# Odd state tiles scaled on ScalarE, added in pairs by adding DMAs; gate and output weights in the expert ring

## The reference

```
x = x + layernorm(mamba(layernorm(x)))      # both directions
x = x + layernorm(moe(layernorm(x)))

branch (once forward, once on the reversed sequence, 512 channels e, 16 states n):
  u     = silu(causal_conv4(x @ W_in[:ED].T))
  delta = softplus(u @ Wx_delta @ Wdt + b_dt);   B, C = u @ Wx_B, u @ Wx_C
  h[t,e,n] = exp(-delta[t,e] * exp(A_log[e,n])) * h[t-1,e,n] + delta[t,e] * B[t,n] * u[t,e]
  y[t,e]   = sum over n of C[t,n] * h[t,e,n]  + D[e] * u[t,e]
mamba = 0.5 * (y_forward + y_backward) * silu(x @ W_in[ED:].T) @ W_out.T

moe: softmax router over 8 experts, top 2; each expert and one shared one:
  gelu(x @ w1 + b1) @ w2 + b2, 256 -> 512 -> 256
```

## Time and profile before

| | |
|---|---|
| median of 3 runs | 4418.58 us (4412.04 to 4423.32) |
| profiled execution, its only recorded time: the span | 4422.2 us |
| PE / DVE / ACT / POOL busy | 3604.0 / 3788.5 / 3101.8 / 3504.8 us |
| mean granted TensorE clock | 0.895 of full speed |
| DMA traffic | 705.06 MB, 159 GB/s over the span |
| chain that ended last, by engine | DVE 29%, PE 25%, POOL 16%, issue 15%, ACT 11% |

### The profile page before, as it was taken

The page is one execution under the profiler, slowest core; times in us unless marked ns, Lnnn a source line. Parts: engine busy times, 40 slices in busy tenths (PEclk is TensorE's granted clock), DMA queues, the critical chain, the costliest instruction groups (busy, mean ns, idle before and its releaser), DMA issues.

```text
span 4422.2 us, 57941 instructions
## 1 busy us (share of the span) xinstructions
PE 3604.0 (81%) x18192; PEld 2562.9 (58%) x18192; DVE 3788.5 (86%) x4688; ACT 3101.8 (70%) x5179; POOL 3504.8 (79%) x2085
## 2 busy tenths in 40 slices
PE   4767596888879887798878887798987989788877
PEld 1444454666546655567555774556655665567656
DVE  3999999898998989899898988989999898989710
ACT  4667576787767876688766887678876787668543
POOL 3898887888878888788887888878887888878611
PEclk7878697999979999899879998899998999889988
DMA  6233142556435663357433674345743565336555
GB/s 196 91 107 104 69 150 75 191 183 214 155 104 172 205 210 130 105 182 245 153 124 131 197 238 147 125 151 194 230 141 107 179 220 188 130 113 204 167 167 182
DMA packets 375805, 705.06 MB, mean 159 GB/s; under 512 B 31937, under 2 KB 205514, under 8 KB 371530
## 3 DMA queue, kind: packets, MB, share of 16 engines
q1 hardware_dynamic: 363210, 667.79, 46.0%
q0 software_dynamic: 12288, 33.57, 2.3%
HBM read 529.82 MB, written 171.44 MB: 159 GB/s over the span
## 4 chain that ended last, share of the span: by engine, by line
DVE 29%; PE 25%; POOL 16%; issue 15%; ACT 11%; DMA 3%; SPq 1%; DVEq 0%; POOLq 0%; ACTq 0%
DVE h L1396 10%; POOL drive L1895 9%; DVE h L1393 7%; DVE y L1405 6%; PE h_t L1170 5%; PE side L1204 4%; PE side L1341 4%; PE side L1333 3%; ACT decay L1610 2%; POOL y L1913 2%; POOL xs_dram L1970 2%; DMA expert_w<-in_w 1%; PE side L1318 1%; DVE stats L1450 1%; POOL work L1982 1%
## 5 line engine op out<-in xcount | busy, mean ns | idle before, releaser
L1895 POOL TENSOR_TENSOR drive<-xu,b_row 128x1024 f32<-128x1024 f32 x960 | 2262.7, 2362 | 386.5 <-DVE h L1396 238.8
L1610 ACT ACTIVATE decay<-delta,neg_a 128x512 f32<-128x512 f32 x2048 | 1401.8, 692 | 747.0 <-DVE h L1396 424.5
L1170 PE MATMUL h_t<-ident,h 128*128 128x128 f32 x8192 | 1332.0, 301 | 523.4 <-DVE y L1405 253.4
L1170 PEld LDWEIGHTS h_t<-ident,h 128*128 128x128 f32 x8192 | 1060.1, 155 | 979.1 <-DVE y L1405 373.1
L1405 DVE SCALAR_TENSOR_TENSOR y<-h_t,c_col,y 128x512 f32<-128x512 f32 x1488 | 1085.9, 730 | 54.0 <-PE h_t L1170 52.9
L1913 POOL TENSOR_TENSOR y<-y,scaled 128x512 f32<-128x512 f32 x496 | 631.8, 1274 | 119.4 <-ACT scaled L1631 118.4
L1396 DVE TENSOR_TENSOR_SCAN h<-decay,h,drive 128x512 f32<-128x512 f32 x512 | 654.1, 1278 | 38.6 <-ACT decay L1610 18.6
L1396 DVE TENSOR_TENSOR_SCAN h<-decay,drive 128x512 f32<-128x512 f32 x512 | 622.0, 1215 | 71.9 <-ACT decay L1610 45.8
L1393 DVE TENSOR_TENSOR_SCAN h<-decay,h,drive 128x512 f32<-128x512 f32 x448 | 573.1, 1279 | 44.7 <-ACT decay L1610 23.1
L1393 DVE TENSOR_TENSOR_SCAN h<-decay,drive 128x512 f32<-128x512 f32 x448 | 544.5, 1215 | 76.4 <-POOL drive L1895 55.7
L1204 PE MATMUL side<-prep_work,conv_diag 128*128 128x512 f32 x960 | 460.9, 605 | 27.3 <-DMA prep_work<-xz_dram 19.3
(11 more groups left out here) (205 smaller groups left out, 4355.7 us busy)
## 6 DMA issues: line engine op xcount, KB each, us to landing
expert_w<-in_w SPq DMA_DIRECT2D x350, 512.0 KB, 4.5
b_row<-b_dram SPq DMA_DIRECT2D x240, 512.0 KB, 4.2
x_dram<-xu SPq DMA_DIRECT2D x16, 2048.0 KB, 7.6
delta_dram<-prep_work SPq DMA_DIRECT2D x64, 512.0 KB, 2.9
delta<-delta_dram SPq DMA_DIRECT2D x64, 512.0 KB, 4.9
ys_dram<-work SPq DMA_DIRECT2D x40, 512.0 KB, 6.5
work<-xs_dram SPq DMA_DIRECT2D x38, 512.0 KB, 4.4
h<-in_w SPq DMA_DIRECT2D x34, 512.0 KB, 5.5
```

The costliest lines, as they stand in the source:

```text
L1170: t = pe.e.transpose(h_t[i % N_H_T][:, c * P:(c + 1) * P], its_h[:, c, :], ident[:, :])
L1610: act.e.activation(decay[:, i % N_DECAY, :], delta[:, c, its], ACT.Exp, scale=neg_a[:, c, w % 2, n:n + 1]).then_inc(decay_made, 1)
L1895: op = pool.e.tensor_tensor(drive[:, k % N_DRIVE, :], xu[:, w % 2, c, :], b_row[:, row % N_B_ROW, :], ALU.mult)
```

## The change

- Every odd tile is scaled by ScalarE, 992 beside the 64 first ones, and the even ones stay with VectorE.
- Two scaled tiles (of y tiles tb-2 and tb, both odd) form a pair in one of three double buffers. GpSimd no longer adds: it issues one DMA for each pair, 496 in all, from SBUF to SBUF with `accum_op` add, of 128 partitions by two rows of 2 KB. It waits for ScalarE's second tile and for the pair before on the same y. Each buffer has a semaphore `added`, and whoever waited for `gathered` waits for it.
- To make room, `w_in_sb` keeps one half and `w_out_sb` goes. For each of the first seven sequences the ring's order begins with the gate half of W_in ("z"), W_out ("out"), and then the shared expert's w1 and w2. For the last one "z" is loaded before the experts of the sequence before, and "out" ahead of their last two w2.
- In `AT` only the places of `const_load` (one fewer) and `ew_load` (16 more loads with the two at slot 0) differ; every other row is just broken differently into lines. In the last sequence the shared w1 and w2 have place 33352 in place of 32608 and 32624; the last `out_mm` is at 33344 and the first `h1_mm` at 33392.

```diff
-N_SCALED = 2
+N_SCALED = 3
-POOL_TILES = (2, 6, 10, 14)
+PAIR = 2
...
         def by_pool(i):
-            return i % (2 * TB) in POOL_TILES or is_first(i)
+            return i % 2 == 1 or is_first(i)
...
+        def pair_with(i):
+            return (of_pool[i] - 1) // PAIR
+        def wait_added(engine, pair):
+            engine.wait_ge(added[pair % N_SCALED], 16 * (pair // N_SCALED + 1))
...
             def scale_tile(i):
...
-                    if at >= N_SCALED:
-                        act.wait_ge(gathered, at - N_SCALED + 1)
-                    into = scaled[:, at % N_SCALED, :]
+                    if pair >= N_SCALED:
+                        wait_added(act, pair - N_SCALED)
+                    into = scaled[:, pair % N_SCALED, at, :]
...
-            def pool_tile(i):
+            def add_pair(i):
                 tb = state_of(i)[2]
-                at = gathered_to(i) - 1
                 pool.wait_ge(tile_scaled, pooled_to(i))
+                wait_y(pool, i - 2)
                 wait_y(pool, i)
-                pool.e.tensor_tensor(y[:, tb, :], y[:, tb, :], scaled[:, at % N_SCALED, :], ALU.add
-                                     ).then_inc(gathered, 1)
+                pool.e.dma_start(out=y[:, tb - 2:tb + 1:2, :], in_=scaled[:, pair_with(i) % N_SCALED, :, :],
+                                 accum_op=ALU.add).then_inc(added[pair_with(i) % N_SCALED], 16)
...
-                if 0 <= i < NW * TILES and by_pool(i) and not is_first(i):
-                    pool_tile(i)
+                if 0 <= i < NW * TILES and i % (2 * PAIR) == 2 * PAIR - 1 and not is_first(i):
+                    add_pair(i)
...
+    ew_order = []
+    for b in range(NB):
+        ew_order += [(b, kind, None) for kind in ("z", "out") if b < NB - 1] + [(b, "w1", None), (b, "w2", None)]
+        if b == NB - 2:
+            ew_order.append((NB - 1, "z", None))
+        for blocks in groups:
+            ew_order += [(b, "w1", j) for j in blocks] + [(b, "w2", j) for j in blocks]
+        if b == NB - 2:
+            ew_order.insert(-2, (NB - 1, "out", None))
...
-        w_in_sb = sb("w_in_sb", [P, DC, 2 * ED])
+        w_in_sb = sb("w_in_sb", [P, DC, ED])
-        w_out_sb = sb("w_out_sb", [P, EC, D])
-        scaled = sb("scaled", [P, N_SCALED, ED])
+        scaled = sb("scaled", [P, N_SCALED, PAIR, ED])
...
+                        if its_kind == "z":
+                            sp.wait_ge(done["z_mm"], nth("z_mm", pb, NH - 1, EC - 1))
+                        elif its_kind == "out":
+                            sp.wait_ge(done["out_mm"], nth("out_mm", pb, TB - 1))
```

More of the change, by code:

```diff
@@ L577, in norm_parts @@
     return NH if b == NB - 1 else 1
-CONSTS = ("chan", "w_in", "wx0", "wdt0", "wx1", "wdt1", "w_out", "router_w", "router_b", "b1", "b2")
+CONSTS = ("chan", "w_in", "wx0", "wdt0", "wx1", "wdt1", "router_w", "router_b", "b1", "b2")
 def by_halves(b, EC, NH):
@@ L687, in side_work @@
         "eo_copy": ("act", lambda b: [(b, g, q) for g in range(NH) for q in range(0, QB, 2)]),
-        "ew_load": ("sp", lambda b: [(i,) for i in range(b * loads + 2, (b + 1) * loads + 2)]),
+        "ew_load": ("sp", lambda b: [(i,) for i in range(b * loads + 2, b * loads + loads + (2 if b < NB - 1 else 0))]),
         "xs_load": ("sp", lambda b: [(b, G) for G in range(NG)]),
@@ L732, in mamba_moe @@
     SLOTS = NG * GROUP
[L733 to L736 removed]
+    ew_order = []
[7 more added lines that the diff above has]
+            ew_order.insert(-2, (NB - 1, "out", None))
+    loads = len(ew_order) // NB
     ew_at = {what: i for i, what in enumerate(ew_order)}
@@ L916, in mamba_moe @@
         tile_scaled = sem("tile_scaled")
-        gathered = sem("gathered")
+        added = [sem(f"added{i}") for i in range(N_SCALED)]
         b_row_in = [sem(f"b_row_in{i}") for i in range(N_B_ROW)]
@@ L1077, in wait_tile @@
             else:
-                engine.wait_ge(gathered, gathered_to(before))
+                wait_added(engine, pair_with(before))
         def ew_place(i):
@@ L1104, in weights_in @@
         def weights_in(pe, b, kind, j):
-            i = b * loads + ew_at[kind, j]
+            i = ew_at[b, kind, j]
             place, which_load = ew_place(i)
@@ L1253, in side_piece @@
                     s, q = divmod(tb, QB)
-                    pe.wait_ge(const_in["w_out"], 16)
+                    wo = weights_in(pe, b, "out", None).rearrange("p (c n) -> p c n", n=D)
                     pe.wait_ge(done["gate"], nth("gate", b, s, EC - 1))
                     for c in range(EC):
-                        mm = pe.e.matmul(bank[:, 0:D], z_of(b, s)[:, c, q * P:(q + 1) * P], w_out_sb[:, c, :],
+                        mm = pe.e.matmul(bank[:, 0:D], z_of(b, s)[:, c, q * P:(q + 1) * P], wo[:, c, :],
                                          start=(c == 0), stop=(c == EC - 1))
@@ L1619, in scale_tile @@
                 b, d = divmod(w, 2)
-                at = gathered_to(i) - 1
+                pair, at = pair_with(i), (of_pool[i] - 1) % PAIR
                 act.wait_ge(turned, i + 1)
@@ new lines, in transfer @@
+                    if kind == "z":
+                        src = w_in_t[:, ED:2 * ED]
+                    elif kind == "out":
+                        src = w_out_t
+                    elif j is None:
+                        src = (w1 if kind == "w1" else w2)[NX - 1]
+                    else:
+                        sp.wait_ge(done["slots"], nth("slots", b))
+                        expert = sp.e.value_load(owner_i[0:1, j:j + 1], min_val=0, max_val=E - 1)
+                        src = (w1 if kind == "w1" else w2)[bass.ds(expert, 1), :, :].rearrange("a k n -> (a k) n")
@@ L2308, in sp_program @@
                 sp.wait_ge(x_out[k], 16 * NB)
+            for i in range(N_SCALED):
+                wait_added(sp, of_pool[-1] // PAIR - 1 - i)
             for tb in range(TB):
```

191 lines of the change are left out of this document (87 added, 104 removed), and 400 rows, old and new, of the table AT.

## The result

The changed kernel takes 4791.9 us (median of 4 runs, 4781.2 to 4799.8), the kernel before, on the same chip, 4421.0 us. The ratio is 1.084 [1.082, 1.087]: 372 us slower, where 85 us faster were forecast and the range ended at 4510.

A forecast was written before the change was run, and what follows sets the result against it. VectorE was taken to bound quiet stages, with other engines nearly full elsewhere. Stage gains of -126 us plus 41 us for batch ends, tail and adding traffic gave -85 us: 4334 us, own range 4290 to 4385, overall 4235 to 4510.

The forecast's parts named there:

- the terms of the quiet cycle: Quiet scan stages: scaling 0.675 us, issue 1.3 us, landing within 7 us, four slots near 6.1 us instead of 6.76.
- dear in the sense of its rival: Quiet cycle's GpSimd: an issue beyond 2.04 us lengthens its four slots; at 2.6 us, 4570 us in all; chance 0.15.
- the sum over the stages, −98 and −28: Scan stages, each limited by its next engine at 98%: -98 us over seven batches, -28 us in the first batch.
- the change does nothing that shows: Rival: ScalarE's 5.4 us more a stage delays its decays as much as VectorE gains; 4418 us; chance 0.08.
- decays more than 100 us late to the scans: Sign of a wrong forecast: decays reach the scans late by more than 100 us in total.
- +24 us for the adding traffic: Four expert stages of each batch: later loads hold up expert matmuls, 0.9 us for each of 28 stages.
- a rival at 0.17: DMA engines fill, expert weights come late, the four expert stages stretch by +81 to +130 us; 4435 us; chance 0.17.
- a bound of 60: Sign of full DMA engines: TensorE's waits for expert weights pass 60 us in all.
- no stall: Last window, four tiles a state: previous pair four slots, 7 us or more, back, longer than a landing of about 4.5 us.
- batch ends, 14 us: Seven batch ends: y dumps wait 3 us later for a landing; 2 us a batch taken, bounds 0 and 5.
- GpSimd's load stays as it was: GpSimd: 496 adds of 1.274 us give way to 496 DMA issues priced at 1.3 us each.
- the ring: Weights through the ring: 14 more 512 KB loads, an SP issue of 0.4 us each; only +3 us at the tail.

The follow-up runs named there:

- e11: The e1 kernel with one extra ScalarE multiply into an unread buffer for every fourth tile; ratio 1.0177, 78 us over the kernel before.
- e13: As e11, with TensorE also waiting for that multiply before refilling the tile's buffer; ratio 1.0222, 98 us over the kernel before.
- e5: The changed kernel without the adds: ScalarE scales the odd tiles, GpSimd neither adds nor issues for them; 4513.7 us, ratio 1.0215.
- e1: The kernel before with only the weights moved through the ring, tiles routed and added as before; 4439.5 us, ratio 1.0044.
- ladder: Five kernels leading from the kernel before to the changed one, the difference between two rungs pricing what was put in; changed kernel at 1.0842.
- e3: The changed kernel with its DMAs copying instead of adding: same bytes written, target not read; 4639.7 us, ratio 1.0495.
- e2: The changed kernel with each adding DMA carrying 16 of 512 columns, the same 496 issues; 4602.1 us, ratio 1.0404.
- e6: The changed kernel with 16-column adding DMAs and the last state of each of the first seven sequences summed by VectorE alone; ratio 1.0316.

## Why the prediction was wrong

**Right: the terms of the quiet cycle.** ScalarE's scaling took 0.681 us (forecast 0.675), the issue 1.21 us in the median (1.3), a pair landed in 6.3 us (within 7), the cycle came to 6.09 us and the next to 5.90 (6.1). Issue and landing are medians: the issue's mean was 1.354 us and the longest landing 13.8. The issue was not dear in the sense of its rival. The Trainium skill ("SBUF — State Buffer", section "SBUF: two separate sides") says that GpSimd cannot write a DMA's descriptors while VectorE runs in a two-port mode. The median issue gives no sign of it, and VectorE's sum took 0.733 us beside 496 issues, 0.730 without. But single issues took up to 3.47 us, and no run here tells why.

**Failed first: the sum over the stages, −98 and −28.** The step was "what stops it next, and no engine filled above 98%". It took a stage as a tank that can be filled. e11 shows that 309 us more on ScalarE cost 59 us although its decays had 747 us of waits. Those waits lie before decays that VectorE's scans release; elsewhere scans and transposed tiles came late all the same (29 and 18 us more waiting in e11). That it is the long side pieces which make them late is my reading, not shown. e13 adds 20 us (uncertain by 17) for tiles that ScalarE holds while it is busy, and TensorE with them. VectorE's relief showed in the quiet stage (54.2 to 48.0 us), but the whole first batch (whose quiet stages I had bound by GpSimd at 49.9 us; 48.2 at 98% are 49.2) took only 13.6 us less in e5 and 2.6 in the changed kernel, where −28 was forecast, and later batches lost: batches 2 to 6 are in e5 on average 13.9 us longer each than in e1 (the sum of the differences in the table, times 32), where −14 was forecast. That the sizes agree is chance; the sign was the error. Of the rivals "the change does nothing that shows" named this mechanism and priced it at equal gain and loss, which was still too kind. The sign that I had named, decays more than 100 us late to the scans, came with 329.5 us, but it was a poor one: the kernel before had 113.6 already.

**Failed worst in size: +24 us for the adding traffic.** The ladder puts the bytes at 193 us, some 40 for writing and 153 for the target's reading, with a border between them that e3's cheaper issues blur. Some 33 of them are at batch ends and some 33 at the end of the kernel. I had the mechanism as a rival at 0.17, with +81 to +130, and gave my own forecast a quarter of that. The Trainium skill ("Collectives: The Full Stack", section "The bandwidth ceiling: the fold count and why AG ≠ RS ≠ AR") says that in a ring between cores ReduceScatter, which adds, reads two sources and so runs at about half AllGather's rate. Within one core's SBUF e3 against the changed kernel agrees, 1.39 us of the engines to 3.05, and the rule deserved to be the likeliest case, since the earlier trace rows showed a stage at 0.89 already. The rival had the place right: from e2 to the changed kernel the four expert stages, 160, 192, 224 and 0, grow by 0.082, 0.096, 0.215 and 0.201 us a slot, 19.0 us a batch of 24.8, and seven batches make 133 us, where its far end was 130. What it left out is the stage at 64 (+0.145, 4.6 us a batch) and the end of the kernel, below. The sign that I had named for it came: TensorE's matmuls of line 1345 waited 88.8 us for expert weights, against a bound of 60, and 34.8 in e2. These 54 us are under a third of 193. Other loads land later too (delta after 6.5 us, 4.6 in e2), and the matmuls of line 1215 waited 53.6 us for their input (41.3 in e2); which of them pays how much is open.

**Failed without being priced: "no stall" in the last window.** Its states have four tiles each, so every pair goes to the same two y tiles and waits for the pair before. I set four slots, 7 us, against a landing of 4.5. The landing took 6.3 us, with an issue of 1.2 before it. GpSimd waited 47.1 us for pairs, 45.0 of them in the last window, which took 279.7 us from first to last scan (245.8 before, 256.6 in e2). Behind the last scan, at 4517.21, the chain that ended last (start, us, what) hangs on one landing after the other:

```profile
4508.05 11.21 DMA y<-scaled
4519.31 0.54 issue
4519.86 5.09 DMA y<-scaled
4524.99 0.58 issue
4525.57 5.20 DMA y<-scaled
4530.81 0.58 issue
4531.39 5.06 DMA y<-scaled
```

GpSimd could start its last issue only 19.9 us after the last scan, and the gathers queued behind it 21.4 us after; in the kernel before its last add started after 6.9 us and the gathers after 8.3. From the last scan to the end the changed kernel takes 281.4 us, e2 271.4, the kernel before 266.3. So 33 of the 193 us of bytes lie in the last window and behind it.

**Mis-sized: batch ends, 14 us.** They measured 39 us with tiny DMAs, 72 with full ones. The dump waits for the pair of the last state, and this for ScalarE's second tile; 3 us for a landing was only the last link. SP waited 130.5 us in 13 times, up to 14.8 us, where 3 us a batch were forecast.

**Missed: the issue's cost where GpSimd has work.** "GpSimd's load stays as it was" is right for the page (3504.8 and 3500.8 us). But the issues and what they do to the drives (2.36 to 2.60 us in the mean) cost some 38 us, give or take 17, over a GpSimd that waits and issues nothing. An add in their place was not set against them in this ladder, so this is not the loss over the kernel before.

**Too low: the ring.** 19 us in all (13 to 26), where traffic and issues were put at nothing and the tail at 3. Where the other 16 come from was not tried. The tail's wait came as forecast: in the changed kernel TensorE waited 2.34 us for the w1 that takes w_out's buffer, though in e1 the time from the last scan to the end grew by 0.8 us only.

```profile
4582.48 0.89 SPq L2271 DMA_DIRECT2D expert_w<-in_w  x2
...
4586.13 5.37 PE L1310 MATMUL side<-xn_t,expert_w 128*128 128x512 f32 x8 [2.34 <-DMA expert_w<-in_w]
```

**Open.** Why odd tiles cost 113 us in the kernel before; how the 45 us of e6 divide exactly between wait and issue (the intervals are about 15 us each); why an adding issue lengthens drives and a copying one does not; how the 193 us divide exactly between writing and adding; and how much of the bytes' price runs through which load or through TensorE's lower clock.

## What to carry to other kernels

Price work moved to DMA by engine time as well as by landing: an SBUF add here took 3.05 us of all sixteen engines for 512 KB, 2.2 times a copy, and three quarters of what the bytes cost in a late batch fell on the four stages with the busiest DMA engines. Where one DMA waits for the landing of another, compare the distance with the landing under load, not with one from a quieter kernel. An engine that waits is not an engine that is free: put the extra load on it alone, as a dummy, before believing a stage table. Where a gain holds only in one phase, make the change in that phase alone: that version gave the 13 us that the full one turned into a loss of 372.

## What the runs showed of the hardware

- An adding DMA of 512 KB within SBUF took 3.05 us of the sixteen engines, the same as a copy 1.39, and 16 KB in 256 rows still 0.51.
- Beside the 12288 packets of gathers and scatters, 496 adding DMAs made 134912 packets on q0, 272 each, and 496 copies of the same bytes 71424, 144 each. The copy's issue on GpSimd was shorter too: 0.753 us in the mean against 1.354.
- The adding issue's record is as long for 16 KB (1.361 us) as for 512 KB (1.354): the bytes don't count in it.
- The landing of a 512 KB add within SBUF took 6.3 us in the median, 5.0 at least and 13.8 at most.
- GpSimd's issue and its elementwise work overlap in the record. With adding issues the drives are longer, 2.60 us in the mean and up to 5.05; with copying ones they are not, 2.36 in the mean and 2.40 at most.
